# Two stages of a transformer kernel joined with the attentions that follow them, without a barrier between

## The chip, the cores and the metric

The kernel runs on 1 core of one Trainium2 chip. Its engines are TensorE (PE), VectorE (DVE), ScalarE (ACT), GpSimd (POOL) and SyncE (SP), which here issues every DMA. The time is that of the whole program on the device, in microseconds (us).

## What is computed

Two post-layernorm transformer layers on x of 8 x 512 x 128 (batch, positions, channels), 16 heads of 8 channels each. The reference, cut to what matters:

```
# layer 0: attention with relative positions
scores = einsum(Q, K) * scale + take(c2p, rel_pos) + swap(take(p2c, p2c_pos))
ctx = softmax(scores) @ V;  x = layernorm(x + ctx @ Wo.T + bo)
# layer 0: gated feed-forward over x and the x of one position earlier
x = layernorm(x + sigmoid(xr @ W_r) * (square(relu(xk @ W_k)) @ W_v))
# layer 1: attention with shifted sinusoids
scores = (QK' + u K' + rel_shift(Q r' + v r')) / sqrt(8)
x = layernorm(x + (softmax(scores) @ V) @ Wo + bo)
# layer 1: four hidden products with silu and gelu
x = layernorm(x + ffn(x))
```

## The kernel before

The program is five stages in a row, each a block of one instruction stream per engine: `opening_phase` (projections of layer 0), `attention_phase(0)`, `mixing_phase` (end of the first attention, feed-forward of layer 0, projections of layer 1; "dense part" in the change's name), `attention_phase(1)` and `dense_phase`. Between two stages stand `end_phase` and `start_phase`: all engines meet, SyncE clears every semaphore of the old stage (L89) and raises every one of the new stage by BASE (L81), and all engines meet again. In the program's order SyncE has 65, 48, 67 and 32 such clears at the four borders.

The opening stage goes over the 8 batches. PE projects a batch to queries, keys and values, ACT and DVE split the results into three bf16 parts, and SyncE writes them to DRAM: values (`write_values`, L169), stacks of the parts (`write_stack`, L174 and L177), offsets (L182), tables (L188). From the fourth batch on it also loads the stacks, tables and offsets of the first eight heads into `a_stks` and `a_tabs` (L193, L194, L232 to L235). Two buffers `o_part` hold the parts, so the next but one batch waits for a batch's writes (`stack_out`).

An attention goes over 128 heads (8 batches of 16), eight of them unrolled in a loop body. Per head and 128-row tile: PE makes scores in PSUM (L703, L705, in layer 0 also L709), DVE adds a band of position terms (L835) and takes the row maximum (L843), ACT exponentiates (L906), PE turns the tile (L724), ACT copies it (L913), PE weighs the values (L737). The band takes a way through DRAM that shifts each row. In layer 0: PE makes the key side (L744), DVE copies it (L853), SyncE writes it with one pitch (`shear_a`, L553) and reads it with another (L559), PE adds its turned form and the query side (`correction`, L751 and L752), ACT copies (L925), SyncE writes and reads again (`shear_b`, L565 and L571). In layer 1: PE makes the edges (L761), DVE copies them (L848), SyncE writes and reads (`shear_e`, L577 and L584). The band chain runs 5 to 7 heads ahead of the scores (`CORR_AHEAD`, `KEY_AHEAD`), the load of stacks 8 heads ahead. Before the first score, the chains of the first heads run alone.

The mixing stage is a pipeline of four batches: step i works on batches i+3, i+2, i+1 and i. Its last part (`tail`) rotates and splits the projections of batch i (L1380 to L1392 on DVE, L1237 and L1242 on ACT) and SyncE writes them: `write_stacks`, 15 DMAs a batch, for each of three groups of terms one for the keys (L1051) and four for query arrays (L1057), with rows of 512 bf16 elements. ACT's cast of the next but one batch waits until they have landed (`stack_written`).

What sets the order is the text of the program: each engine runs its stream in order, and SyncE has one queue. A DMA waits on that queue for the semaphore of its input, and everything behind it waits too.

## Time and profile before

| what | value |
|---|---|
| median of 3 runs (lowest, highest) | 2052.94 us (2052.21, 2053.58) |
| profiled execution, its time | 2053.05 us |
| its span, first to last instruction | 2051.2 us |
| PE, DVE, ACT busy | 84%, 71%, 72% of the span |
| DMA | 404.65 MB, 197 GB/s over the span |
| opening stage | 4.8 to 105 us, with the barrier behind it |
| first attention | 105 to 907 us |
| mixing stage | 907 to 1092 us |
| second attention | 1092 to 1704 us |
| dense stage | 1704 to 2051 us |

The spans of the stages are read from the first instruction behind each barrier. Busy time is summed over an engine's instructions; waits on semaphores, DMA issues and the clears and raises of semaphores are not in it, so a border between stages shows as time in which no engine is busy.

### The profile page before, as it was taken

To read this page: it belongs to the slowest core of one execution; us is meant where nothing else is said; L and a number is where in the kernel's file an instruction comes from. 1 tells how busy PE (TensorE), PEld (TensorE's weight loads), DVE (VectorE), ACT (ScalarE), POOL (GpSimd) and SP (SyncE) were. 2 spreads that over 40 slices of the span, in tenths; PEclk is the share of its full clock that TensorE was granted. 3 is DMA by queue.
4 is the path that set the end of the run, shared out by engine and by line. 5 is a ranking of instruction groups with operands and counts; after the bars stand their busy time and mean duration, and the time that the engine had idled before them with its cause. 6 is when DMAs were issued, how large, how long until landed. Compare 5 with 4: busy or idle time off the path is not lost. (4 is left out here: it accounts for less than half of the span.)

```text
span 2051.2 us, 44474 instructions
## 1 busy us (share of the span) xinstructions
PE 1728.5 (84%) x11694; PEld 1042.4 (51%) x11694; DVE 1454.1 (71%) x3499; ACT 1472.5 (72%) x2600; POOL 79.9 (4%) x102
## 2 busy tenths in 40 slices
PE   5269999999999999946743999999999995999998
PEld 2045555555555555524522555656565552454544
DVE  6358888888888888837973888988888873324322
ACT  4348888888888888836862999999999991223222
POOL 0000000000000000003510000000000000000000
PEclk8569999999999999977875999999999997999999
DMA  7678888888888888726996777777777744000100
GB/s 229 214 222 257 265 269 267 264 261 266 262 264 268 266 266 261 240 56 184 327 311 182 206 213 210 215 211 214 212 211 211 212 136 117 22 20 26 36 5 11
DMA packets 428234, 404.65 MB, mean 197 GB/s; under 512 B 38169, under 2 KB 348433, under 8 KB 428049
## 3 DMA queue, kind: packets, MB, share of 16 engines
q1 hardware_dynamic: 428177, 403.99, 65.6%
q8 instruction: 24, 0.39, 0.1%
...
HBM read 227.09 MB, written 176.29 MB: 197 GB/s over the span
## 5 line engine op out<-in xcount | busy, mean ns | idle before, releaser
L906 ACT ACTIVATE a_prob<-bank,a_negmax 128x512 f32<-128x512 f32 x1024 | 740.8, 723 | 47.3 <-DVE a_negmax L843 46.1
L843 DVE TENSOR_REDUCE a_negmax<-bank 128x1 f32<-128x512 f32 x1024 | 699.4, 683 | 0.3
L724 PE MATMUL bank<-a_ident,a_prob 128*128 128x128 f32 x4096 | 643.0, 280 | 56.2 <-ACT a_probt L913 48.3
L913 ACT COPY a_probt<-bank 128x512 f32<-128x512 f32 x1024 | 621.3, 607 | 90.4 <-PE bank L724 79.1
L724 PEld LDWEIGHTS bank<-a_ident,a_prob 128*128 128x128 f32 x4096 | 448.5, 141 | 171.7 <-issue 70.6
L835 DVE TENSOR_TENSOR bank<-bank,a_band 128x128 f32<-128x128 f32 (+3 forms) x1024 | 349.9, 342 | 69.6 <-PE bank L705 69.0
L703 PE MATMUL bank<-a_stks 74*128 74x192 bf16 (+7 forms) x1024 | 324.1, 317 | 10.4 <-ACT a_prob L906 10.1
L737 PE MATMUL bank<-a_probt,a_vs 128*32 128x512 f32 x2048 | 271.5, 604 | 14.9 <-ACT a_probt L913 14.9
L823 DVE COPY_PREDICATED bank<-a_mask,bank 128x128 f32<-128x128 uint32 (+1 forms) x512 | 139.6, 273 | 116.4 <-PE bank L709 114.0
L703 PEld LDWEIGHTS bank<-a_stks 74*128 74x128 bf16 (+1 forms) x1024 | 100.1, 98 | 235.3 <-ACT a_prob L906 200.4
L705 PE MATMUL bank<-a_stks 74*128 74x320 bf16 (+5 forms) x768 | 200.9, 262 | 0.0
L1676 DVE TENSOR_TENSOR d_drop<-bank,d_s 128x128 f32<-128x128 f32 x32 | 7.1, 284 | 170.4 <-PE bank L1599 170.4
L709 PE MATMUL bank<-a_stks 74*128 74x128 bf16 (+1 forms) x512 | 110.5, 216 | 10.9 <-DVE bank L823 2.6
L1578 PE MATMUL bank<-d_ha,d_h1T 128*128 128x512 f32 x256 | 112.3, 592 | 0.0
L751 PE MATMUL bank<-a_ident,a_sheared 128*128 128x128 f32 x512 | 106.4, 285 | 6.6 <-DMA a_sheared<-shear_a 5.1
L1578 PE MATMUL bank<-d_hb,d_h2T 128*128 128x512 f32 x256 | 111.2, 592 | 0.0
L925 ACT COPY a_corr<-bank 128x512 f32<-128x512 f32 x128 | 76.4, 597 | 42.9 <-PE bank L752 40.1
L848 DVE COPY a_corr<-bank 128x512 f32<-128x512 f32 x128 | 87.2, 681 | 16.7 <-PE bank L761 9.3
L752 PE MATMUL bank<-a_tabs,a_stks 65*128 65x128 bf16 x512 | 97.5, 225 | 0.0
L853 DVE COPY a_keyside<-bank 128x512 f32<-128x512 f32 x128 | 87.4, 683 | 13.3 <-PE bank L744 10.4
L761 PE MATMUL bank<-edges,a_stks 96*128 96x128 bf16 x512 | 51.0, 223 | 50.1 <-DMA a_ident<-in_ident 42.5
L1641 ACT ACTIVATE d_hb<-bank,d_fs 128x512 f32<-128x512 f32 x32 | 22.0, 687 | 90.6 <-PE bank L1578 90.6
...
## 6 DMA issues: line engine op xcount, KB each, us to landing
a_band<-shear_b SPq DMA_DIRECT2D x128, 512.0 KB, 5.0
shear_a<-a_keyside SPq DMA_DIRECT2D x128, 256.0 KB, 3.7
a_sheared<-shear_a SPq DMA_DIRECT2D x128, 256.0 KB, 3.7
shear_b<-a_corr SPq DMA_DIRECT2D x128, 256.0 KB, 2.8
shear_e<-a_corr SPq DMA_DIRECT2D x128, 256.0 KB, 2.2
a_band<-shear_e SPq DMA_DIRECT2D x128, 256.0 KB, 3.2
a_stks<-stack SPq DMA_DIRECT2D x256, 96.0 KB, 3.0
...
```

The costliest lines, as they stand in the source:

```text
L703: last = pe.matmul(score[:, 0:c], k[:, qlo, q], k[:, keys, 0:c], start=True, stop=True)
L705: last = pe.matmul(score[:, c:T], k[:, qhi, q], k[:, keys, c:T], start=True, stop=True)
L709: last = pe.matmul(other[:, 0:e - a], k[:, qhi, q], k[:, keys, a:e], start=True, stop=True)
L724: last = pe.transpose(turned_bank[k][:, n * 128:(n + 1) * 128], prob[h.slot % 2][:, n, k * 128:(k + 1) * 128], ident[:, :])
L737: pe.matmul(cbank[32 * j:32 * j + VW, :], vs[g][:, at:at + VW], probt[h.slot + j][:, k, :], start=(k == 0), stop=(k == NT - 1)).then_inc(p ...
L751: pe.matmul(corr_bank[:, q], sheared[h.slot % 4][:, q], ident[:, :], is_transpose=True, start=True, stop=False)
L823: v.copy_predicated(score[:, a:e], mask[:, 0:e - a], other[:, 0:e - a]).then_inc(fixed, 1)
L835: v.tensor_tensor(score[:, a:e], score[:, a:e], band[h.slot % bands][:, n, w:w + e - a], ALU.add).then_inc(added, 1)
L843: v.tensor_reduce(negmax[h.slot % 2][:, n:n + 1], score[:, :], AX.X, ALU.max, negate=True).then_inc(maxed, 1)
L906: nc.scalar.activation(prob[h.slot % 2][:, n, :], score[:, :], ACT.Exp, bias=negmax[h.slot % 2][:, n:n + 1]).then_inc(exped, 1)
L913: nc.scalar.copy(probt[h.slot][:, k, :], turned_bank[k][:, :]).then_inc(copied, 1)
L1578: last = pe.matmul(dst[:, :], w[:, k, 128 * m:128 * m + 128], src[:, k, :], start=(k == 0), stop=(k == KH - 1))
```

## The change

`opening_phase` and `mixing_phase` become `opening` and `mixing`, which no longer make a block of their own: each gives a program that is put into the same block as the attention behind it, engine by engine. The two `end_phase` and `start_phase` between them fall away; the semaphores of both are raised together ahead of the pair and cleared together behind it (SyncE then has 112 and 109 clears at the borders in front of the mixing and the dense stage). Buffers that only the stage ahead needs share memory (`arena`) with `prob` and `probt` of the attention.

The first heads' chains are written into the stage ahead. In the opening: stack and table loads from the fourth batch on, the products of key sides 0 to 3 after batches 5 and 6, their way through shear_a in batches 6 and 7, corrections after the last offset product. In mixing: stack loads of heads 0 to 7 behind batches 2 to 5 (two heads a batch), edges 0 and 1 in step 5 and 2 to 4 in step 6, all copied by ACT instead of DVE, and their writes and reads in steps 6 and 7. The stacks of the last mixing batch are written behind the first four heads of the second attention (`store_last`), and `settled` waits for all of the stage's writes after the fourth head.

Three more things: `stack1` has a row pitch of 5 x 512 + 32 elements and its query arrays are written as one row of 2049 elements instead of four of 512, 6 DMAs a batch for 15; the load of two rotated arrays is two pieces of 512 elements instead of one of 1024; and the second attention has 8 buffers each for edges and bands instead of 2 and 4.

The diff, cut to its core:

```diff
-ARRAYS = 5
+PITCH_S = 5 * T + 32
...
                     for b in range(B):
                         write_values(b)
+                        if b == 7:
+                            for j in (0, 1):
+                                att.shear_a_read(sp, j)
                         write_stack(b)
...
-                            if b > 3:
-                                first_head(2 * (b - 4))
-                                first_head(2 * (b - 4) + 1)
+                        if b > 2:
+                            for j in ((0, 1, 2), (3, 4), (5, 6), (), (7,))[b - 3]:
+                                att.head_load(sp, j)
+                        if b == 6:
+                            sp.wait_ge(filled, BASE + 16 * N_FILL)
+                            for j in (0, 1):
+                                att.shear_a_write(sp, j)
+                            att.offset_load(sp, 0)
+                        if b == 7:
+                            for j in (2, 3):
+                                att.shear_a_write(sp, j)
...
                     for b in range(B):
                         offset_product(b)
                         if b + 2 < B:
                             project(b + 2)
+                        if b == 5:
+                            pe.wait_ge(w_off_set, BASE + 2)
+                            for j in (0, 1):
+                                att.first_key(pe, j)
+                        if b == 6:
+                            for j in (2, 3):
+                                att.first_key(pe, j)
+                    pe.wait_ge(off_set, BASE + B)
+                    att.first_correction(pe, 0)
...
-            wide, bands = WIN if rel else REL, 4
+            wide, bands, corrs = (WIN, 4, 2) if rel else (REL, 8, 8)
...
+            def write_keys(sp, b):
+                sp.wait_ge(lo_set, BASE + 2 * b + 2)
+                for first_term, n, q in TERM_RUNS:
+                    sp.dma_start(stack[1][b, :, first_term:first_term + n, 0:T], part[b % 2][:, 0:n, KEYS:KEYS + T]).then_inc(stack_written[b % 2], 16)
+            def write_queries(sp, b, run):
+                sp.wait_ge(lo_set, BASE + 2 * b + 2)
+                first_term, n, q = TERM_RUNS[run]
+                same = bass.AP(part[b % 2][:, :, :].tensor, q * (WIDE + 2) + QV, [[3 * (WIDE + 2), C], [0, n], [1, 4 * T + 1]])
+                sp.dma_start(stack[1][b, :, first_term:first_term + n, T:5 * T + 1], same).then_inc(stack_written[b % 2], 16)
...
                         if tail is not None:
                             write_values(tail)
-                            write_stacks(tail)
+                        if tail == 6:
+                            for j in range(CORR_AHEAD - 1):
+                                att.edge_read(sp, j)
+                        if tail == 7:
+                            att.edge_read(sp, CORR_AHEAD - 1)
+                        if tail is not None and tail < B - 1:
+                            write_keys(sp, tail)
+                            for run in range(len(TERM_RUNS)):
+                                write_queries(sp, tail, run)
...
+                        if tail in (2, 3, 4, 5):
+                            att.head_load(sp, 2 * tail - 4)
+                            att.head_load(sp, 2 * tail - 3)
...
-            opening_phase(*kept)
-            end_phase()
-            attention_phase(0, kept)
-            end_phase()
-        mixing_phase()
+            start_phase()
+            with nc.Block() as block:
+                first.program(block)
+                att.program(block, first)
         end_phase()
...
+                mix.program(block)
+                att.program(block, mix)
```

Where the instructions stand now. SyncE's queue at the end of the opening stage and the start of the first attention, before (L182 offsets, L193 and L194 head loads, L89 the clears, L637 the mask, L553 and L559 write and read of shear_a):

```order
L182 DMA offsets<-o_off_part 4x16x1536
L193 DMA a_stks<-stack 48x2x512
L194 DMA a_stks<-stack 48x512
L193 DMA a_stks<-stack 48x2x512
L194 DMA a_stks<-stack 48x512
L182 DMA offsets<-o_off_part 4x16x1536
L89 ISA x65
L637 DMA a_mask<-in_mask 128x128
L553 DMA shear_a<-a_keyside 128x512 x2
L559 DMA a_sheared<-shear_a 128x512
L553 DMA shear_a<-a_keyside 128x512
```

After, from the last batch's values on (L599 and L600 are the head loads, L625 and L631 write and read of shear_a):

```order
L199 DMA values<-o_vt 128x4x144
L631 DMA a_sheared<-shear_a 128x512 x2
L204 DMA stack<-o_part 128x3072
L207 DMA stack<-o_part 128x1536
L207 DMA stack<-o_part 128x1024
L207 DMA stack<-o_part 128x512
L212 DMA offsets<-o_off_part 4x16x1536
L599 DMA a_stks<-stack 48x2x512
L600 DMA a_stks<-stack 48x512
L625 DMA shear_a<-a_keyside 128x512 x2
L631 DMA a_sheared<-shear_a 128x512 x2
L212 DMA offsets<-o_off_part 4x16x1536
```

The writes and reads of the first key sides stand between the last batch's own writes, no clear stands between them, and one head load is left there instead of four.

ACT in the mixing step of batch 6, before (L1258 rows of the last batch, L1237 and L1242 casts, L1210 a query copy):

```order
L1258 ACTIVATE m_x<-m_pre,m_shift,m_rstd 128x128 x4
L1237 CAST m_part<-m_full 128x1024
L1270 COPY m_xt<-bank 128x512
L1242 CAST m_part<-m_left 128x1538
L1210 ACTIVATE m_qv<-bank,m_uvs 128x512
```

and after (L722 are the copies of the first edges):

```order
L1367 ACTIVATE m_x<-arena,m_shift,m_rstd 128x128 x4
L722 COPY a_corr<-bank 128x512 x2
L1346 CAST m_part<-arena 128x1024
L1379 COPY arena<-bank 128x512
L722 COPY a_corr<-bank 128x512 x2
L1351 CAST m_part<-arena 128x1536
L722 COPY a_corr<-bank 128x512
L1319 ACTIVATE arena<-bank,m_uvs 128x512
```

Five copies of edges stand between the step's own instructions. SyncE's queue behind the last mixing step, before (L1051 and L1057 stacks of the three groups of terms, L532 to L535 the loads of head 0):

```order
L1051 DMA stack<-m_part 128x3x512
L1057 DMA stack<-m_part 128x3x512 x4
L1051 DMA stack<-m_part 128x2x512
L1057 DMA stack<-m_part 128x2x512 x4
L1051 DMA stack<-m_part 128x512
L1057 DMA stack<-m_part 128x512 x4
L89 ISA x67
L532 DMA a_stks<-stack 48x1536
L533 DMA a_stks<-stack 48x512
L534 DMA a_stks<-stack 48x512
L535 DMA a_stks<-stack 48x1024
```

and after, from the start of the attention's own part (L649 write of edges, L656 read of a band, L604 to L607 loads of a head, L1087 query rows of the last batch):

```order
L649 DMA shear_e<-a_corr 128x4x128
L604 DMA a_stks<-stack 48x1536
L605 DMA a_stks<-stack 48x512
L606 DMA a_stks<-stack 48x512
L607 DMA a_stks<-stack 48x2x512
L1087 DMA stack<-m_part 128x3x2049
L649 DMA shear_e<-a_corr 128x4x128
L656 DMA a_band<-shear_e 128x4x128
L604 DMA a_stks<-stack 48x1536
L605 DMA a_stks<-stack 48x512
L606 DMA a_stks<-stack 48x512
L607 DMA a_stks<-stack 48x2x512
```

The last batch's writes have moved behind the attention's own DMAs of its first heads, whose earlier loads stand several batches ahead.

## Rows read from the trace of the kernel before

**Rows 1.** Busy time by stretch: span, then engines, PE clock, DMA share, GB/s.

```profile
450.00:550.00 100.00, 93.34 (x740) 58.26 (x740) 85.54 (x220) 86.67 (x156) 0.00 (x0) 1.00 0.89 267
985.00:1000.00 15.00, 12.90 (x58) 9.17 (x58) 13.61 (x31) 11.94 (x22) 7.37 (x9) 0.77 1.00 334
1330.00:1430.00 100.00, 93.86 (x781) 59.92 (x780) 87.68 (x200) 98.13 (x185) 0.00 (x0) 1.00 0.73 212
1069.00:1083.00 14.00, 0.00 (x0) 0.00 (x0) 0.00 (x0) 0.00 (x0) 0.00 (x0) 0.50 1.00 342
85.00:88.00 3.00, 0.00 (x0) 0.00 (x0) 0.00 (x0) 0.00 (x0) 0.00 (x0) 0.50 1.05 387
```

**Rows 2.** Timeline, end of the opening: start us, us, engine, line, what [idle before].

```profile
82.11 0.68 DVE L372 TENSOR_TENSOR o_off_part<-o_off_left,o_off_part 64x512 bf16<-64x512 f32 x1 [0.68 <-ACT o_off_part L319]
83.87 0.43 SPq L169 DMA_DIRECT2D values<-o_vt  x1
...
92.56 0.54 SPq L182 DMA_DIRECT2D offsets<-o_off_part  x1
```

**Rows 3.** Timeline, start of the first attention.

```profile
105.51 0.58 PE L744 MATMUL bank<-a_stks,a_tabs 65*128 65x512 bf16 x1 [27.00 <-SPq L635]
108.27 1.73 SPq L553 DMA_DIRECT2D shear_a<-a_keyside  x2
110.34 0.32 SPq L559 DMA_DIRECT2D a_sheared<-shear_a  x1
...
117.32 0.44 SPq L553 DMA_DIRECT2D shear_a<-a_keyside  x1
121.22 0.32 SPq L559 DMA_DIRECT2D a_sheared<-shear_a  x1
...
125.65 0.45 PE L751 MATMUL bank<-a_ident,a_sheared 128*128 128x128 f32 x1 [2.90 <-DMA a_sheared<-shear_a]
126.95 0.37 PE L703 MATMUL bank<-a_stks 74*128 74x192 bf16 x1
129.56 0.69 ACT L906 ACTIVATE a_prob<-bank,a_negmax 128x512 f32<-128x512 f32 x1 [1.77 <-DVE a_negmax L843]
```

**Rows 4.** Marks of both barrier halves, L85 behind clears, L77 behind raises: times us.

```profile
L85 POOLq DRAIN  x4: 34/34/41, 97.6 to 1699.6; - x4
L85 SPq DRAIN  x4: 7/7/7, 101.6 to 1701.8; - x4
L77 POOLq DRAIN  x5: 34/34/41, 0.7 to 1702.0; - x5
L77 SPq DRAIN  x5: 7/7/7, 4.5 to 1704.1; - x5
```

**Rows 5.** Timeline of SP, ACT and DVE, end of the mixing stage.

```profile
1031.49 0.37 SPq L1051 DMA_DIRECT2D stack<-m_part  x1
...
1046.52 0.37 SPq L1051 DMA_DIRECT2D stack<-m_part  x1
...
1050.26 1.04 ACT L1237 CAST m_part<-m_full 128x1024 bf16<-128x1024 f32 x1 [0.83 <-DVE m_full L1381]
...
1060.15 1.47 ACT L1237 CAST m_part<-m_full 128x1538 bf16<-128x1538 f32 x1 [1.46 <-DMA stack<-m_part]
...
1065.49 2.90 DVE L1392 TENSOR_TENSOR m_part<-m_left,m_part 128x1538 bf16<-128x1538 f32 x2 [0.41 <-ACT m_part L1242]
...
1081.71 2.19 SPq L1057 DMA_DIRECT2D stack<-m_part  x4
```

**Rows 6.** Timeline of SP, PE and DVE, start of the second attention.

```profile
1092.38 0.35 SPq L532 DMA_DIRECT2D a_stks<-stack  x1
...
1100.53 0.61 PE L761 MATMUL bank<-edges,a_stks 96*128 96x128 bf16 x4 [42.49 <-DMA a_ident<-in_ident]
...
1112.68 0.49 DVE L835 TENSOR_TENSOR bank<-bank,a_band 128x128 f32<-128x128 f32 x2
```

**Rows 7.** The page's groups: ACT's copy of a correction in the first attention.

```profile
L925 ACT COPY a_corr<-bank 128x512 f32<-128x512 f32 x128 | 76.4, 597 | 42.9 <-PE bank L752 40.1
```

2312 lines of the change are left out of this document (1185 added, 1127 removed).

## The prediction

> **What bounds the kernel now.** I read the table by stretches first: how busy each engine is in one window of each stage [rows 1]. In the first attention (450 to 550 us) ACT and DVE are 87 and 86% busy, PE 93%; in the second (1330 to 1430 us) ACT is 98% busy. In the mixing stage (985 to 1000 us) DVE is busy 13.6 of 15 us and the DMA share is 1.00. So each stage is near a limit of its own and the change touches none of these loops' arithmetic. What is left is the seams, and there I read the timeline, at the two places where a stage ends and an attention starts.
>
> Seam one: the last engine work of the opening stage is a DVE instruction that ends at 82.8 us, SyncE's last DMA of that stage is issued at 92.6 [rows 2], and the attention's first product starts at 105.5, its first exponential at 129.6 [rows 3]. That is 46.8 us between the last engine work of one stage and the first exponential of the next. Seam two: DVE's last work of the mixing stage ends at 1068.4, SyncE still queues stack writes until 1083.9 [rows 5], the attention's first DMA is issued at 1092.4, its first product starts at 1100.5 and DVE adds the first band at 1112.7 [rows 6]. That is 44.3 us. Both together are 91 us, 4.4% of the run.
>
> **What the barriers cost, and what of that stays.** A barrier is three things here: waiting until the last DMA has landed, clearing every semaphore of the old stage, and raising every semaphore of the new one by BASE. The change keeps the number of semaphores nearly the same: SyncE's instructions show 65, 48, 67 and 32 clears before and 112 and 109 after. The clears are one instruction each and they are not hidden. From the queue's own marks [rows 4]: the first barrier's 65 clears run from 97.6 to 101.6 us, 4.0 us; the last one's 32 from 1699.6 to 1701.8, 2.2 us; so (4.0 - 2.2) / 33 = 0.055 us a clear. The first 65 raises run from 0.7 to 4.5 us, 3.8 us, the last 36 from 1702.0 to 1704.1, 2.1 us: 1.7 / 29 = 0.059 us a raise; I take 0.055 for both. This work does not vanish with the barrier, it moves:
> - ahead of the opening stage, 112 raises for 65: 47 x 0.055 = +2.6 us
> - after the first attention, 112 clears for 48: 64 x 0.055 = +3.5 us
> - ahead of mixing, 109 raises for 67: 42 x 0.055 = +2.3 us
> - after the second attention, 109 clears for 32: 77 x 0.055 = +4.2 us
>
> Together +12.6 us (9 to 15 at 0.04 to 0.065 us each), all on the path, since every engine waits at these barriers. The seams below are reckoned without them.
>
> **Seam one.** SyncE's queue is what is late here. In the last batch it issues values, four stacks, offsets, four head loads and offsets, 11 DMAs, from 83.9 us to 93.1 [rows 2], 0.84 us each. In the new order the same stretch up to the write of the fourth key side holds values, two reads of shear_a, four stacks, offsets, two head loads and two writes of shear_a: 12 DMAs, 10.1 us. Of the batches before it only batch 6 has another number of DMAs, two writes and three offset loads for four head loads, +0.8 us; batch 3 has six head loads in place of six offset loads. So values is issued at 84.7, the third key side is written at 93.1 and the fourth is out at 94.8. The engines' part is hidden under this queue: key products and DVE's key copies go where DVE waits for ACT and ACT for stack writes. The read of the third key side waits until its write has landed: 2.1 us from issue to issue in the trace (108.27 to 110.34 us) [rows 3], so about 95.2; two reads, an offset write and a write of shear_b, 0.3 to 0.5 us each as the issues of [rows 2, 3], put the fifth key side's write at 96.9. From there the old start-up chain is unchanged and I take it whole: write of that key side at 117.32, its read at 121.22, the fifth correction on PE at 125.65, the first score at 126.95, the first exponential at 129.56 [rows 3], 12.2 us. The first exponential comes at 109.1 instead of 129.6: -20.4 us. Bounds: if the whole start-up from the first write of shear_a (108.27 to 129.56, 21.3 us) ran only after the old queue's end at 93.1, it would come at 114.4: -15.2. If the read waits hid entirely, -25.
>
> **Seam two.** Nothing of the second attention waits for the seam any more: stacks of the first eight heads are loaded behind batches 2 to 5, their edge products and ACT's copies lie in batches 5 and 6, the last batch's stacks are written behind the first four heads. The score tiles of the first head can run as soon as PE has finished its projections; then DVE adds the first band right behind its last mixing instruction, ahead of which only the ACT additions push. Those are five copies of one bank, 0.597 us each by the same copy in the first attention [rows 7], 3.0 us, put into the step of batch 6. In that step ACT waited 0.83 us for DVE ahead of one cast and 1.46 us for stack<-m_part ahead of another [rows 5]. The first wait takes up 0.8 us of the copies; of the second I count half, since the writes that it waits for start as late as before. I take +1.5 us (0 to 3.0). Then the first band is added at 1068.4 + 1.5 = 1069.9 instead of 1112.7: -42.8 us. The activation table for the exponential is loaded while DVE finishes its last 2.9 us, as it now lies behind ACT's last cast. The last batch's 3.9 MB (15 DMAs of 128 rows and 512 elements each, 6 parts and 5 arrays) come on top of the attention's 212 GB/s at a DMA share of 0.73 [rows 1]; four heads at 4.5 us leave 18 us for 3.8 + 3.9 MB, which takes 22 us at 342 GB/s, the rate of pure stack writes [rows 1]. The 4 us fall into loads that are issued eight heads ahead and bands that are issued five ahead: cover of over 15 us, cost nothing.
>
> In the mixing steps themselves each of batches 2 to 5 gets eight head loads (0.67 MB). A step is 15.0 us long, from one batch's first stack write to the next (1031.5 to 1046.5) [rows 5]. Its DMA is 3.93 MB of stacks, 0.55 of values and rows, now 0.67 of heads: 5.15 MB. The trace bounds the rate: 342 GB/s where all rows are 1 KB, 387 GB/s in the opening's writes with rows of 1 to 6 KB [rows 1]. That is 15.1 or 13.3 us, and the new query rows are 4 KB. Batches 1 and 2, which also carry the next loads, need 5.64 and 6.08 MB: 16.5 and 17.8 us or 14.6 and 15.7. I take no cost, nearer to the fast rate; the other end is 79.6 us of DMA for five steps of 75, +5 us.
>
> A rule speaks against the new rows. The Trainium skill, page DMA: Bandwidth & Descriptors, section How a descriptor splits into AXI transactions, says that a row which does not start at a multiple of 256 bytes costs extra beats: a 576-byte one 25 in place of 18. The old pitch of 5120 bytes is such a multiple, the new one of 5184 is not. By that rule a 1 KB row would cost up to a quarter more, a 4 KB row about 6%: estimates from the page, of which no row of this trace shows anything; they would make the step 15.8 us of DMA and add some 3 us to the mixing stage.
>
> **Loops.** The bodies are the same instructions. With 9.25 ACT instructions a head the first runs 156 / 9.25 heads in 100 us, 5.93 us each, the second with 8.25 of them 4.46 [rows 1]. Eight buffers for edges and bands loosen waits of DVE and SyncE in the second attention, where ACT has 98% of the time: at most its idle 1.9 us in 100, over 580 us some 10, and I count none.
>
> **The sum**, against the profiled execution's 2053.05 us (span 2051.2; the median of the runs, 2052.94, is 0.1 lower): 2053.05 + 12.6 - 20.4 - 42.8 = 2002.4, taken as 2002.5 us, 2.5% faster. Extremes added: +9 - 25 - 44.3 = 1993 and +15 - 15.2 - 41.3 + 5 = 2016.5.
>
> **Rivals.**
> - Mixing gets bound by DMA. The share of 1.00 at 985 to 1000 us speaks for it, the 387 GB/s with long rows against. Price +5 us for the stage, and ACT's wait for stack writes grows by 1 to 3 us: 2008 to 2011.
> - Seam one only moves: SyncE's single queue holds the stage's own writes behind waits for landed key sides, and the start-up chain runs after it as before. For it: the queue has no gap in the last batches. Price: -15.2 for -20.4, 2008.
> - The second attention's loop gets a little faster, by ACT's idle time: 1992 to 1998. Against: no wait of ACT there is for a band.
> - Slower: the head loads of the second attention, now 1 KB pieces that start off the 256-byte grid and two pieces where one of 2 KB was, become so dear that DMA sets the loop. The loop uses 0.73 of DMA [rows 1], 3.25 us of a head's 4.45; the loads are 48 rows of 7 KB, 336 of the 945 KB that 212 GB/s move in a head's time, 1.2 us. To lose the 50.5 us gained, a head must take 0.4 us more, 4.85 us of DMA, so the loads would have to cost 2.8, 2.35 times as much. At three times as much the head takes 5.6 us: 2002.5 + 128 x 1.15 = 2150. The rule above gives a quarter more for them, 3.55 us a head, which changes nothing.
> - The change doesn't do what it says: the attention's first tiles wait after all until SyncE has written batch 6, because the bands' reads stand in that queue. They stand ahead of batch 6's stacks, so I give it little: at most 12 us of writes, 2014.
>
> **How the numbers follow.** Forecast 55%, with a range of its own of 1996 to 2009; mixing bound by DMA 17%; seam one only moved 11%; faster loop 8%; bands late 6%; slower 3%. Leaving out the slower case and the tails of the others, 1992 to 2015 holds 8 in 10. What a measurement here can tell from no change is about 0.2%, 4 us; all cases but the slower one lie more than 30 us below: faster 96%, within 0.2% 1%, slower 3%.
>
> **What would show it.** In the profile after: 112 and 109 clears, some 6 to 7 us each; the first exponential near 112 us of the new clock (109.1 + 2.6), the second attention's first band within 2 us of DVE's last mixing instruction, in place of 44.3; ACT's copies of a_corr in batch 6; stack writes with 4 KB rows during the first four heads of the second attention; mixing steps of 15 us; loops of 5.93 and 4.46 us a head as before. I am wrong if these loops change by over 1%, if the mixing steps are longer than 16 us, or if the exponentials of the second attention start later than 5 us after DVE's last mixing instruction.

## The result, and the profile after

The changed kernel takes 2017.95 us (median of 4 runs, 2013.47 to 2020.02) against 2053.01 before: a ratio of 0.9825, 95% interval 0.9811 to 0.9839. It is faster, as forecast, but by 35 us and not by 50.5. The 2002.5 us are missed by 15.5 us and the upper end of the range, 2015, by 3. The profiled execution took 2019.39 us with a span of 2017.6. Of all runs below one, the fourth of e2, took 2138.4 us at a granted TensorE clock of 0.78 instead of 0.95, and no median below has it.

A table by stretch says where. The marks are events that both traces have: the first DMA, the first exponential of the first attention, its last copy of outputs, the first DMA of the mixing stage, the first band added in the second attention, its last copy of outputs, the first DMA of the dense stage, the end; each mark is the start of its event. All are us.

| stretch | before | after | difference | forecast |
|---|---|---|---|---|
| raises ahead of the opening | 4.8 | 8.0 | +3.2 | +2.6 |
| opening to first exponential | 124.8 | 111.1 | -13.7 | -20.4 |
| rest of first attention | 767.1 | 765.7 | -1.4 | 0 |
| border to mixing | 10.6 | 16.9 | +6.3 | +5.8 |
| mixing to first band | 205.5 | 165.0 | -40.5 | -42.8 |
| rest of second attention | 583.9 | 591.2 | +7.3 | 0 |
| border to dense | 7.8 | 12.1 | +4.3 | +4.2 |
| dense | 346.9 | 347.7 | +0.8 | 0 |

The differences add to -33.6 us, which is that of the spans. (The forecast of -42.8 has 1.5 us of ScalarE's copies in it.) So 6.7 us are missing in the opening, of which the first attention returns 1.4, 7.3 in the first heads of the second attention, 2.3 in mixing, 1.2 in the semaphores, 0.8 in the dense stage: 16.9 us, what lies between 2019.39 and 2002.5. The dense stage spans 346.7 to 348.6 us in all the profiles below, so I read nothing into its 0.8.

The borders first, which answer to [rows 4]. Marks of both barrier halves of the changed kernel, L85 behind the clears, L77 behind the raises; first and last start:

```profile
L85 POOLq DRAIN  x2: 34/38/41, 887.9 to 1660.9; - x2
L85 SPq DRAIN  x2: 7/7/7, 894.5 to 1667.4; - x2
L77 POOLq DRAIN  x3: 34/34/41, 0.7 to 1667.6; - x3
L77 SPq DRAIN  x3: 7/7/7, 7.7 to 1669.7; - x3
```

112 clears run from 887.9 to 894.5 us, 109 from 1660.9 to 1667.4, and 112 raises from 0.7 to 7.7. That is 0.06 us each, 0.005 over what I took.

Seam one, answering to [rows 3]. Timeline of SyncE and ScalarE in the changed kernel; start, duration, what, and the idle time before it with what ended it:

```profile
97.60 0.83 SPq L625 DMA_DIRECT2D shear_a<-a_keyside  x2
101.97 0.95 SPq L631 DMA_DIRECT2D a_sheared<-shear_a  x2
...
103.63 0.39 SPq L637 DMA_DIRECT2D shear_b<-a_corr  x1
...
110.57 0.59 ACT L752 COPY a_corr<-bank 128x512 f32<-128x512 f32 x1 [11.98 <-DMA shear_b<-a_corr]
112.79 0.59 ACT L752 COPY a_corr<-bank 128x512 f32<-128x512 f32 x1 [1.64 <-PE bank L740]
116.76 0.59 ACT L752 COPY a_corr<-bank 128x512 f32<-128x512 f32 x1 [3.39 <-PE bank L740]
119.11 0.69 ACT L949 ACTIVATE arena<-bank,a_negmax 128x512 f32<-128x512 f32 x1 [1.76 <-DVE a_negmax L898]
```

A hop is one step of the chain through DRAM: the issue of a DMA, its landing, and the release of what waits for it. The fourth key side's write is out at 98.4 us, 98.0 by the forecast on this clock; the third's is issued at 97.60, where the forecast has 96.3. Then the read of the third waits until 101.97, 4.4 us after the write's issue, where I had 2.1. The first write of shear_b goes out at 103.63, and ScalarE, idle for 11.98 us in all, can copy the third correction only when it has landed, since there are two correction buffers: 6.9 us from issue to landing, 3.7 in the kernel before (116.84 to 120.5). The first exponential comes at 119.1, not 112.3.

Seam two, answering to [rows 5, 6]. ScalarE and VectorE at the end of mixing and the start of the second attention:

```profile
1048.97 1.50 ACT L1351 CAST m_part<-arena 128x1536 bf16<-128x1536 f32 x1
1052.41 0.59 ACT L722 COPY a_corr<-bank 128x512 f32<-128x512 f32 x1 [1.95 <-PE bank L713]
...
1064.82 1.28 ACT L949 ACT_TABLE_LOAD   x1
1067.81 2.28 ACT L949 ACTIVATE arena<-bank,a_negmax 128x512 f32<-128x512 f32 x3 [1.71 <-DVE a_negmax L898]
...
1055.71 1.23 DVE L1511 TENSOR_TENSOR m_part<-arena,m_part 128x1024 bf16<-128x1024 f32 x1 [3.46 <-ACT m_part L1351]
...
1063.88 2.89 DVE L1511 TENSOR_TENSOR m_part<-arena,m_part 128x1536 bf16<-128x1536 f32 x2 [0.40 <-ACT m_part L1351]
1066.69 0.49 DVE L890 TENSOR_TENSOR bank<-bank,a_band 128x128 f32<-128x128 f32 x2
```

The seam itself closed as forecast: VectorE adds the first band (L890) directly behind its last mixing instruction, and the exponential table is loaded meanwhile. In the step of batch 6, ScalarE waits 1.95 us for the product of the fifth edge tile ahead of its copy (L722), and VectorE 3.46 us for ScalarE. One earlier step is longer too. ScalarE and VectorE in the changed kernel, between the rotations of batches 3 and 4:

```profile
1011.21 1.47 ACT L1346 CAST m_part<-arena 128x1536 bf16<-128x1536 f32 x1 [1.85 <-DMA stack<-m_part]
...
1021.20 0.69 DVE L1480 TENSOR_TENSOR arena<-bank,arena 128x512 f32<-128x512 f32 x1 [3.95 <-PE bank L1246]
```

ScalarE waits 1.85 us until the stacks of batch 2 have landed, and VectorE, behind ScalarE and TensorE, 3.95 us. In the same step of the kernel before the waits are 0.23 and 1.67 us. The step lasts 17.8 us where it lasted 15.5; the other steps up to batch 5 last 14.9 to 16.4 us (15.0 to 16.3 before). It is 17.8 and 17.9 us in e1 and e7, and 18.7 in e10.

Then the first heads, by stretches of 20 us from the first band on, with the columns of [rows 1] (length of the stretch; busy us and instructions of PE, PEld, DVE, ACT and POOL, PEld being TensorE's weight loads; granted clock; DMA share; GB/s):

```profile
1066.00:1086.00 20.00, 16.06 (x91) 10.56 (x92) 17.99 (x42) 16.26 (x30) 0.00 (x0) 0.73 0.96 343
1086.00:1106.00 20.00, 16.31 (x130) 10.05 (x128) 12.46 (x29) 15.83 (x30) 0.00 (x0) 1.00 0.90 271
1106.00:1126.00 20.00, 17.34 (x131) 10.23 (x132) 16.50 (x38) 17.53 (x33) 0.00 (x0) 0.91 0.75 206
```

and the same from the kernel before:

```profile
1112.00:1132.00 20.00, 16.75 (x97) 10.45 (x95) 18.17 (x43) 16.64 (x30) 0.00 (x0) 0.76 0.68 177
1132.00:1152.00 20.00, 19.16 (x159) 12.19 (x158) 17.55 (x41) 19.73 (x38) 0.00 (x0) 1.00 0.68 197
1152.00:1172.00 20.00, 18.49 (x151) 11.60 (x149) 17.83 (x42) 19.64 (x38) 0.00 (x0) 1.00 0.76 217
```

ScalarE, which sets this loop, is busy 15.8 of 20 us in the second stretch where it was 19.7, and 17.5 in the third where it was 19.6: 6.0 us together. The DMA share is 0.96 and 0.90 in the first two stretches, against 0.68 and 0.68. VectorE's waits say for what:

```profile
1089.43 0.30 DVE L890 TENSOR_TENSOR bank<-bank,a_band 128x128 f32<-128x128 f32 x1 [2.67 <-DMA a_band<-shear_e]
...
1106.01 0.30 DVE L890 TENSOR_TENSOR bank<-bank,a_band 128x128 f32<-128x128 f32 x1 [2.96 <-DMA a_band<-shear_e]
...
1079.94 0.43 SPq L1087 DMA_DIRECT2D stack<-m_part  x1
...
1086.40 1.35 SPq L1087 DMA_DIRECT2D stack<-m_part  x1
...
1088.38 1.01 SPq L656 DMA_DIRECT2D a_band<-shear_e  x1
```

Two bands land late, at 1089 us among the writes of the last batch's stacks (L1087, the one at 1086.40 takes 1.35 us to issue), and at 1106 behind the last of them, issued at 1097.

### The profile page after: what moved, and what is told of

The parts are those of the page before. It is cut to its first block and busy times, and to the rows that moved or that the text cites. A ratio compares the mean times of both kernels' runs of the same rounds, so it can differ in the third digit from the quotient of the medians.

```text
span 2017.6 us, 44338 instructions
## 1 busy us (share of the span) xinstructions
PE 1726.7 (86%) x11694; PEld 1041.8 (52%) x11694; DVE 1447.8 (72%) x3492; ACT 1474.8 (73%) x2605; POOL 79.6 (4%) x102
## 5 line engine op out<-in xcount | busy, mean ns | idle before, releaser
L949 ACT ACTIVATE arena<-bank,a_negmax 128x512 f32<-128x512 f32 x1024 | 739.4, 722 | 34.6 <-DVE a_negmax L898 33.6
L813 PE MATMUL bank<-ident,arena 128*128 128x128 f32 x4096 | 644.3, 280 | 58.4 <-ACT arena L956 50.4
L956 ACT COPY arena<-bank 128x512 f32<-128x512 f32 x1024 | 620.1, 606 | 90.2 <-PE bank L813 77.8
L813 PEld LDWEIGHTS bank<-ident,arena 128*128 128x128 f32 x4096 | 449.7, 141 | 176.4 <-issue 71.4
L890 DVE TENSOR_TENSOR bank<-bank,a_band 128x128 f32<-128x128 f32 (+3 forms) x1024 | 350.0, 342 | 77.2 <-PE bank L794 69.5
L826 PE MATMUL bank<-arena,a_vs 128*32 128x512 f32 x2048 | 272.4, 606 | 14.9 <-ACT arena L956 14.9
L878 DVE COPY_PREDICATED bank<-a_mask,bank 128x128 f32<-128x128 uint32 (+1 forms) x512 | 139.5, 272 | 114.3 <-PE bank L798 112.3
L739 PE MATMUL bank<-ident,a_sheared 128*128 128x128 f32 x512 | 106.2, 285 | 20.4 <-DMA a_sheared<-shear_a 15.2
L1700 PE MATMUL bank<-d_ha,d_h1T 128*128 128x512 f32 x256 | 112.3, 592 | 0.0
L752 ACT COPY a_corr<-bank 128x512 f32<-128x512 f32 x128 | 76.4, 597 | 24.4 <-PE bank L740 12.3
L739 PEld LDWEIGHTS bank<-ident,a_sheared 128*128 128x128 f32 x512 | 74.1, 145 | 35.7 <-issue 23.2
L1768 ACT ACTIVATE d_hc<-bank,d_fs 128x512 f32<-128x512 f32 x32 | 22.0, 687 | 87.6 <-PE bank L1700 87.6
```

The costliest lines, as they stand in the source:

```text
L739: pe.matmul(corr_bank[:, q], sheared[h.slot % 4][:, q], ident[:, :], is_transpose=True, start=True, stop=False)
L813: last = pe.transpose(turned_bank[k][:, n * 128:(n + 1) * 128], prob[h.slot % 2][:, n, k * 128:(k + 1) * 128], ident[:, :])
L826: pe.matmul(cbank[32 * j:32 * j + VW, :], vs[g][:, at:at + VW], probt[h.slot + j][:, k, :], start=(k == 0), stop=(k == NT - 1)).then_inc(p ...
L878: v.copy_predicated(score[:, a:e], mask[:, 0:e - a], other[:, 0:e - a]).then_inc(fixed, 1)
L890: v.tensor_tensor(score[:, a:e], score[:, a:e], band[h.slot % bands][:, n, w:w + e - a], ALU.add).then_inc(added, 1)
L949: nc.scalar.activation(prob[h.slot % 2][:, n, :], score[:, :], ACT.Exp, bias=negmax[h.slot % 2][:, n:n + 1]).then_inc(exped, 1)
```

## The experiments

All are variants of the changed kernel, and e11 and e12 of e10. This is the table by stretch of all profiles (us; "start" is the first DMA; the middle columns are the stretches of the table above):

| | start | to first exp | attention 0 | border | to first band | attention 1 | border | dense | median |
|---|---|---|---|---|---|---|---|---|---|
| changed | 8.0 | 111.1 | 765.7 | 16.9 | 165.0 | 591.2 | 12.1 | 347.7 | 2018.0 |
| e1 | 8.0 | 110.1 | 765.4 | 17.0 | 163.7 | 584.5 | 12.2 | 346.7 | 2009.7 |
| e2 | 8.0 | 108.6 | 765.9 | 16.9 | 163.1 | 584.4 | 12.1 | 348.4 | 2009.3 |
| e3 | 8.0 | 111.8 | 764.9 | 16.9 | 164.5 | 590.6 | 12.1 | 347.8 | 2019.7 |
| e4 | 8.0 | 110.2 | 768.1 | 16.9 | 164.1 | 591.3 | 12.1 | 348.0 | 2016.4 |
| e5 | 8.0 | 100.5 | 768.6 | 16.9 | 164.8 | 590.0 | 12.1 | 348.6 | 2010.6 |
| e6 | 8.0 | 106.5 | 764.5 | 16.9 | 164.7 | 592.0 | 12.1 | 347.0 | 2012.1 |
| e7 | 4.5 | 108.9 | 766.2 | 10.1 | 162.4 | 590.1 | 7.5 | 347.7 | 2001.9 |
| e8 | 8.0 | 109.3 | 764.6 | 16.9 | 187.0 | 584.7 | 12.1 | 348.0 | 2032.3 |
| e9 | 8.0 | 111.4 | 766.8 | 16.9 | 171.5 | 595.2 | 12.1 | 347.3 | 2029.2 |
| e10 | 4.4 | 101.1 | 771.3 | 10.1 | 162.1 | 585.0 | 7.5 | 346.9 | 1987.9 |
| e11 | 4.4 | 100.9 | 772.6 | 10.1 | 161.4 | 586.0 | 7.5 | 348.5 | 1993.3 |
| e12 | 4.4 | 101.3 | 768.3 | 9.8 | 162.3 | 587.9 | 7.5 | 346.9 | 1989.2 |

Where a column's code is the same, its spread is what one profile can't tell apart: 108.6 to 111.4 us for the opening (changed, e1, e2, e4, e7, e8, e9), 163.1 to 165.0 for mixing (changed, e2, e3, e5, e6), 764.6 to 768.1 for the first attention (changed, e1, e2, e4, e7, e8, e9), 590.0 to 592.0 for the second (changed, e3, e5, e6, e7).

### The first heads of the second attention: e1, e2, e8

e1, the last batch's stacks left out (and zeros written there early in mixing):

```diff
-                        if not rel:
-                            before.store_last(sp, j)
```

> The changed kernel, with the stacks of the last mixing batch not written during the first four heads of the second attention; the rows of the last batch hold zeros instead, written by six DMAs early in the mixing stage (so the scores of the last 16 heads lack their data). Theory A (DMA backlog): the first heads of the second attention lose their time because the 3.9 MB of these stacks come on top of batch 6's 3.9 MB and of the attention's own 212 GB/s. Then the stretch from the first band (1066.7 us in the changed kernel) to the end of the attention (1660.9), 594.2 us there and 586.9 us before, shrinks by 5 to 7 us to 587 to 589, the waits of 2.67 and 2.96 us for a band at 1089 and 1106 us go, and the whole is 2011 to 2014 us where the changed kernel has 2018. Rival B (the slow first heads come from TensorE's lower clock and the order of the first tiles, not from DMA): the stretch stays at 593 to 595 us and the time at 2017 to 2019.

2009.7 us. The attention takes 584.5 us from the first band, 6.7 less than in the changed kernel and within 0.6 of the kernel before. e2 writes the same bytes, thinner:

```diff
-                    before.settled(sp)
-                    with sp.Fori(0, loops) as i:
+                    if not rel:
+                        for j in range(unroll):
+                            sync_step(sp, 0, FIRST + j, NHEAD)
+                            before.store_last(sp, FIRST + j)
+                    before.settled(sp)
+                    with sp.Fori(0 if rel else 1, loops) as i:
```

> The changed kernel, with the last mixing batch's stacks written in nine pieces over the first nine heads of the second attention instead of six over the first four (SyncE's first loop iteration written out). Theory A: the backlog spreads; at a DMA share of 0.73 the attention leaves some 92 GB/s of 342 free, 3.9 MB fit into 42 us, nine heads; the stretch from the first band to the attention's end falls from 594.2 us to 588 to 591, the time to 2012 to 2015 us. Rival B: no change, 2017 to 2019 us. If only batch 6's burst of 3.9 MB ahead of the first bands matters, this gains under 2 us while the variant without the last batch's stacks gains under 2 us as well.

584.4 us, 2009.3 us: as good as not writing them at all, and more than expected. Its first three stretches of 20 us:

```profile
1062.00:1082.00 20.00, 16.22 (x101) 10.41 (x102) 18.48 (x45) 17.47 (x31) 0.00 (x0) 0.79 0.96 329
1082.00:1102.00 20.00, 18.92 (x157) 11.88 (x154) 17.39 (x41) 19.73 (x38) 0.00 (x0) 1.00 0.96 298
1102.00:1122.00 20.00, 17.77 (x143) 11.04 (x144) 16.57 (x39) 18.48 (x35) 0.00 (x0) 1.00 0.95 270
```

The DMA share is 0.95 or 0.96 in all three, and ScalarE's second stretch is full again at 19.73. So it is not the bytes that cost 7 us but that they came faster than the loop's own use leaves room for. Theory A holds and B falls. Three more kernels below write these stacks the same way, and their second attention takes 585.0, 586.0 and 587.9 us: 0.5 to 4.0 us over the 583.9 of the kernel before, in four profiles. e8 goes the other way: the heads wait for all writes.

```diff
+                    if not rel:
+                        for j in range(FIRST):
+                            before.store_last(sp, j)
+                        before.settled(sp)
                     for j in range(FIRST):
                         sync_step(sp, 0, j, NHEAD, weighed=False)
-                        if not rel:
-                            before.store_last(sp, j)
...
+                    if not rel:
+                        before.settled(pe)
```

(and the same wait on VectorE and ScalarE)

> The changed kernel, with the waiting of the old barrier put back at seam two, without its clears and raises and with the first heads' chains still in the mixing stage: SyncE writes all stacks of the last batch first, and TensorE, VectorE, ScalarE and SyncE start the second attention when all of them have landed. The backlog is then gone when the heads start. Theory: the first band comes 3.9 + 3.9 MB behind, at 1083 to 1090 us instead of 1066.7, the attention then takes 587 to 588 us instead of 594.2, and the whole is 10 to 17 us slower than the changed kernel, 2028 to 2035 us: what is worth the most in seam two is that the first heads don't wait for the last writes. If the backlog is worth as much as the waiting, the time stays at 2018 to 2022.

2032.3 us. VectorE's first band:

```profile
1085.75 0.63 DVE L895 TENSOR_TENSOR bank<-bank,a_band 128x128 f32<-128x128 f32 x2 [23.65 <-PE bank L797]
```

The first band comes at 1085.8, 22.0 us later in the stretch, and the attention then takes 584.7 us, 6.5 less: 14.4 us of time. The overlap of the last writes is worth 22 us gross and 14 net as the change has it, and 23 with the writes thinned (2032.3 against 2009.3 us in e2).

### Seam one: e3, e5, e6

e3, SyncE doesn't hold its first shear_b writes behind the reads that wait for a landing:

```diff
+                    write_offsets(B - 1)
+                    att.shear_b_write(sp, 0)
+                    att.shear_b_write(sp, 1)
                     for j in (2, 3):
                         att.shear_a_read(sp, j)
-                    write_offsets(B - 1)
-                    att.shear_b_write(sp, 0)
                     att.shear_a_write(sp, 4)
-                    att.shear_b_write(sp, 1)
```

> The changed kernel, with SyncE's order at the end of the opening altered: the last offsets and the writes of the first two corrections to shear_b come before the reads of the third and fourth key side, which wait 3.5 us for a landing, instead of behind them. Theory C (seam one is late because SyncE's queue holds behind landings): the first shear_b write goes out at about 98.5 to 99.5 us instead of 103.6, and since it is what frees the two correction buffers, the first exponential of the first attention comes 3 to 5 us earlier than 119.1 us; time 2013 to 2015 us. Rival D (the chain is bound by DMA landings of 4 to 7 us however they are ordered): the first exponential at 118 to 120 us, time 2017 to 2019.

The first exponential comes at 119.79, time 2019.7: theory C, mine, fell, and rival D holds. The trace shows that the order did what it should, and nothing came of it:

```profile
98.13 1.46 SPq L637 DMA_DIRECT2D shear_b<-a_corr  x2
99.93 3.64 SPq L631 DMA_DIRECT2D a_sheared<-shear_a  x2
...
107.03 0.45 PE L739 MATMUL bank<-ident,a_sheared 128*128 128x128 f32 x1 [10.24 <-DMA a_sheared<-shear_a]
```

The shear_b writes are out at 98.1 to 99.6, some 5 us earlier, but the read of the third key side, issued at 99.93, now takes until 107.03 to reach the correction on TensorE (L739), 7.1 us; it was 101.97 to 104.72 in the changed kernel. What one hop gained, the next lost. The run has one thing besides: the last offsets, too, are now written ahead of the reads, and e6 will show that they matter. e5 takes the stage's own last writes out of the way:

```diff
                     att.shear_b_read(sp, 2)
+                    write_values(B - 1)
+                    write_stack(B - 1)
+                    write_offsets(B - 2)
+                    write_offsets(B - 1)
```

(and leaves them out where they stood)

> The changed kernel, with the opening stage's own last writes (values and stacks of the last batch, offsets of the last two) issued behind the chains of the first heads instead of among them. Theory G (each hop through DRAM in seam one takes 4 to 7 us instead of 2 to 4 because the stage's own writes are in the DMA engines): the hops become 2 to 4.5 us as in the kernel before, and the first exponential comes at 111 to 114 us instead of 116.6 to 119.8; some 1 to 3 us of it are given back in the first heads, where the 2.2 MB now fall: time 2012 to 2015 us. Rival H (hops are long for their own sake, in both kernels): the first exponential moves by under 2 us.

The first exponential at 108.52, more than forecast, and 2010.6 us:

```profile
90.56 0.83 SPq L630 DMA_DIRECT2D shear_a<-a_keyside  x2
93.55 0.94 SPq L636 DMA_DIRECT2D a_sheared<-shear_a  x2
94.60 0.37 SPq L642 DMA_DIRECT2D shear_b<-a_corr  x1
...
98.07 0.58 ACT L757 COPY a_corr<-bank 128x512 f32<-128x512 f32 x1 [2.44 <-DMA shear_b<-a_corr]
...
108.52 0.69 ACT L954 ACTIVATE arena<-bank,a_negmax 128x512 f32<-128x512 f32 x1 [1.76 <-DVE a_negmax L903]
```

Writes and reads of key sides are 3.0 us apart (90.56 to 93.55), ScalarE waits 2.44 us for shear_b, where it was 11.98. The first exponential is 8.0 to 10.8 us earlier than in the kernels with the changed opening (116.56 to 119.36). Of the 10.6 us to the changed kernel's profile 7.0 are SyncE's queue: the third key side is written at 90.56 instead of 97.60, since the values, stacks and offsets that SyncE issued from 89.3 to 95.4 us no longer stand ahead of it. From that write to the first exponential it takes 18.0 us instead of 21.5: 3.5 us are shorter landings and one write of offsets less on the way. In the kernel before, the same stretch takes 18.5 us (111.10 to 129.56). The first attention takes 768.6 us, 2.9 more than in the changed kernel but only 0.5 beyond the spread. e6 moves only the two writes of offsets, 384 of 2200 KB:

```diff
-                        if b > 0:
+                        if 0 < b < 7:
                             write_offsets(b - 1)
...
                     att.shear_b_read(sp, 2)
+                    write_offsets(B - 2)
+                    write_offsets(B - 1)
```

> The changed kernel, with only the writes of the last two batches' offsets (192 KB each) issued behind the first heads' chains. If a few engines of the 16 that carry these writes hold up what stands behind them, the shear_b write that takes 6.9 us to land in the changed kernel takes 3 to 4.5, and the first exponential comes 2 to 4 us earlier, 113 to 116 us. If the volume of all the stage's writes is the cause, under 1 us, 117 to 119.5.

114.45, 2.1 to 4.9 us earlier than with the changed opening, and 2012.1 us, as expected if these small writes hold up what is behind them out of proportion: their own issues are 1.5 us of it. The 1.8 MB of values and stacks are written as before, so volume isn't what costs most of it.

The traces hold one thing more, the single landing events of a DMA, of which what waits needs the last. In the changed kernel a write of 128 rows posts 16 of them, a write of offsets (64 rows of 3 KB) five: one 1.0 to 1.3 us after its issue, the other four 4.3 to 6.7 us after it. The first write to shear_b (us from its issue):

| | before | changed | e5 | e6 |
|---|---|---|---|---|
| eighth of 16 landing events | 3.0 | 2.7 | 3.0 | 3.0 |
| last | 3.7 | 6.9 | 3.4 | 3.6 |

In the seven profiles with the changed opening the eighth comes after 2.4 to 2.7 us and the last after 5.5 to 7.3. So half of a slow write lands as fast as ever and a few parts of it come late, while the last offsets, issued 0.65 us ahead of it in the changed kernel, are still landing (107.3 to 109.7 us; the write's last event is at 110.5). That these few parts share their DMA engines with the offsets fits both and isn't shown directly, as no record names the engine. Theory G holds in the main: the hops are long because of the stage's own writes, and of these it is the two small ones of offsets. From the third key side's write to the first exponential e6 takes 18.6 us, e5 18.0, the profiles of the changed opening 20.6 to 23.1.

### The semaphores and the copy order in mixing: e7

```diff
-                @block.sync
-                def _(sp):
-                    for handle in sems.values():
-                        sp.sem_clear(handle)
+                shares(block, lambda queue, handle: queue.sem_clear(handle))
...
-                        if tail == 6:
-                            att.first_edge_out(act, 4)
...
                             values_out(p)
+                            if tail == 6:
+                                att.first_edge_out(act, 4)
                             high(p, 0)
```

(`shares` gives every fifth semaphore to one of the five engines; the raises likewise)

> The changed kernel with two edits that lie in different places of the trace. One: the semaphores are cleared and raised by all five engines, a fifth each, instead of by SyncE alone. At 0.055 us each on SyncE, 112 take 6.2 us and 23 take 1.3: the two clearings shrink from 6.6 and 6.5 us to 1.5 to 2.5 and the raises from 7.0, some 6 and 2.1 to 2, 2 and 1 us, together 17 to 20 us less. If the semaphores are served one after the other whoever asks, nothing is gained. Two: ACT's copy of the fifth edge tile in the mixing step of batch 6 stands behind the step's own copies of queries and keys instead of ahead of them, where ACT waited 1.95 us for its product: the stretch from the end of the clearing to the first band, 170.4 to 172.2 us in five profiles, less its raises, shrinks by 1 to 2.5 us. Whole: 1998 to 2001 us.

2001.9 us. Start and borders fall by 3.5, 6.8 and 4.6, 14.9 us, less than the 17 to 20 expected, but more than the 13.8 that the change had added: the engines clear and raise at the same time. The second edit, in the step of batch 6:

```profile
1041.05 1.23 DVE L1513 TENSOR_TENSOR m_part<-arena,m_part 128x1024 bf16<-128x1024 f32 x1 [1.39 <-ACT m_part L1353]
```

VectorE waits 1.39 us where it waited 3.46, 2.07 us less (and the same 1.39 or 1.40 in e10 and e12, which have this edit). The kernel before had this step 2.1 us shorter than the changed one (12.04 us between the rotations of batches 5 and 6, 14.14 after), and e7 has 12.06 again. So ScalarE's 3.0 us of copies cost nothing; where one of them stood did, as it put two of TensorE's own products (L1252, L1254) ahead of what ScalarE waited for.

### Layout of stack1: e4, e9

```diff
-PITCH_S = 5 * T + 32
+PITCH_S = 5 * T + 128
```

> The changed kernel, with a pitch of stack1's rows of 5 x 512 + 128 elements, 5376 bytes, a multiple of 256, instead of 5184, which is none. Theory E (rows that start off the 256-byte grid cost more, as the Trainium skill has it, page DMA: Bandwidth & Descriptors, section How a descriptor splits into AXI transactions): the mixing stage, 165.1 us from its start to the first band in the changed kernel, gets 1 to 3 us shorter, and the DMA share of the second attention's loop falls from 0.73 by 0.02 or more. Rival F (the grid costs nothing here): 164.5 to 165.5 us and 0.73, time 2017 to 2019 us.

164.1 us to the first band, inside the spread, and a DMA share of 0.75 in the loop where it was 0.73: rival F. A pitch off the 256-byte grid costs nothing here that a run can tell, with query rows of 4 KB; query rows of 1 KB at both pitches were not compared.

e9 undoes the long rows:

```diff
-                same = bass.AP(..., q * (WIDE + 2) + QV, [[3 * (WIDE + 2), C], [0, n], [1, 4 * T + 1]])
-                sp.dma_start(stack[1][b, :, first_term:first_term + n, T:5 * T + 1], same)...
+                for at in range(0, 4 * T, T):
+                    wide = T + (at == 3 * T)
+                    same = bass.AP(..., q * (WIDE + 2) + QV + at, [[3 * (WIDE + 2), C], [0, n], [1, wide]])
+                    sp.dma_start(stack[1][b, :, first_term:first_term + n, T + at:T + at + wide], same)...
```

> The changed kernel, with the query arrays of stack1 written in four pieces of 512, 512, 512 and 513 elements each, 15 DMAs a batch as before, instead of one row of 2049. Pitch and contents are the changed kernel's. If long rows keep the mixing steps, which now carry the head loads too, from being bound by DMA (1 KB rows moved 342 GB/s, rows of 1 to 6 KB 387 in the kernel before), the stretch from the mixing stage's first DMA to the first band, 163.1 to 165.0 us in the profiles so far, grows by 3 to 8 us, and the backlog behind it costs the first heads 1 to 2 us more: 2022 to 2028 us. If the long rows do nothing, 163 to 165.5 us and 2016 to 2020.

2029.2 us, 11 more and 1 beyond what I expected: 6.5 in mixing and 4.0 in the second attention. Both kernels in mixing, the changed one first:

```profile
1006.00:1021.00 15.00, 9.59 (x50) 7.31 (x48) 11.18 (x22) 10.23 (x18) 8.54 (x8) 0.77 1.06 363
1021.00:1036.00 15.00, 10.74 (x51) 7.02 (x50) 11.92 (x20) 12.84 (x22) 4.85 (x4) 0.89 0.94 334
```

```profile
1006.00:1021.00 15.00, 7.62 (x37) 5.12 (x36) 12.11 (x27) 8.83 (x16) 8.54 (x8) 0.77 1.03 307
1021.00:1036.00 15.00, 9.04 (x41) 5.62 (x40) 12.01 (x20) 12.21 (x21) 4.99 (x4) 0.80 0.94 301
```

In these stretches the DMA moves 301 and 307 GB/s with rows of 512 elements and 334 and 363 with rows of 2049; in the other full stretches of e9 it moves 319 to 332 (981 to 996 us, 323; 997 to 1012, 332; 1016 to 1031, 319; 1033 to 1048, 329). ScalarE then waits for the stacks' landing step by step:

```profile
1014.13 1.47 ACT L1348 CAST m_part<-arena 128x1536 bf16<-128x1536 f32 x1 [3.82 <-DMA stack<-m_part]
...
1047.68 1.47 ACT L1348 CAST m_part<-arena 128x1536 bf16<-128x1536 f32 x1 [1.54 <-DMA stack<-m_part]
...
1065.07 2.42 ACT L1348 CAST m_part<-arena 128x1536 bf16<-128x1536 f32 x2 [3.42 <-DMA stack<-m_part]
```

e9's short rows start off the 256-byte grid, unlike those of the kernel before. How much of the 11 us is the rows' length and how much their start isn't separated: that takes e9 at the pitch of e4, which wasn't run.

### Together: e10, e11, e12

e10 is e2, e5 and both edits of e7 in one kernel.

> Four edits of the runs so far together: the opening's own last writes behind the first heads' chains, the mixing stage's last stacks over nine heads, all five engines clearing and raising semaphores, the fifth edge copy later. They lie in different stretches, so the table by stretch should add: 4.5 to the first DMA, 100.5 to the first exponential, 768.6, a border of 10.1, 162.4 to 164, 584.4, a border of 7.5, 347.5, in all 1985.5 to 1987 us of span, 1987 to 1990 us of time. If one edit's gain was only moved behind (the backlog of one stretch met in the next), more than 1992.

1987.9 us, a ratio of 0.968 to the kernel before (0.9664 to 0.9697) and 30 us under the changed one. The stretches add up, but for the first attention: 771.3 us, 5.6 more than in the changed kernel and 2.6 more than in e5, which writes the same there. In e11 the opening's last writes go out in pieces behind each of the first four heads.

```diff
                         sync_step(sp, 0, j, NHEAD, weighed=False)
-                        if not rel:
-                            before.store_last(sp, j)
+                        before.store_last(sp, j)
...
+                    def store_last(sp, j):
+                        if j == 0:
+                            write_values(B - 1)
+                            write_offsets(B - 2)
...
```

> As the joined kernel, with the opening's own last writes in pieces behind each of the first four heads of the first attention instead of all at once ahead of them. In the variant with these writes in one piece the first attention took 768.6 us from its first exponential where five profiles of the changed opening show 764.9 to 768.1. If the burst of 2.2 MB costs the first heads 1 to 3 us, pieces bring 766 to 767 and the whole is 1 to 2 us below the joined kernel; if not, the same within 1 us.

1993.3: worse, 5.4 us above e10, against the forecast. The first attention takes 772.6 us, 1.3 more than in e10; the rest of the 5.4 isn't explained. The stall only moved (second and fourth stretch of 10 us, from the first exponential on; e10 first, e11 second):

```profile
115.50:125.50 10.00, 6.57 (x56) 4.92 (x53) 7.39 (x20) 7.62 (x15) 0.00 (x0) 0.98 0.76 239
135.50:145.50 10.00, 9.31 (x74) 5.44 (x73) 8.34 (x22) 8.57 (x16) 0.00 (x0) 1.00 0.94 286
```

```profile
115.40:125.40 10.00, 8.87 (x72) 6.48 (x71) 9.91 (x26) 9.69 (x19) 0.00 (x0) 1.00 0.92 299
135.40:145.40 10.00, 6.33 (x49) 3.85 (x47) 5.88 (x16) 6.16 (x11) 0.00 (x0) 0.92 0.66 208
```

VectorE, 9.7 of 10 us busy there in the changed kernel's second stretch, is 7.4 in e10, and 5.9 in e11's fourth. e12 has pieces of 128 to 288 KB over eleven heads.

```diff
+                    bounds = {3: (0, 2), 4: (2, 3), 5: (3, 5), 6: (5, 6), 7: (6, 8), 8: (8, 9), 9: (9, 11), 10: (11, 12)}
...
+                            for a, at, src in terms[slice(*bounds[j])]:
+                                sp.dma_start(stack[0][B - 1, a, :, at, :], part[(B - 1) % 2][:, src, :])...
```

> The joined kernel, with the opening's own last writes cut into pieces of 128 to 288 KB over the first eleven heads of the first attention (SyncE's first loop iteration written out there too). In the joined kernel this attention takes 771.3 us from its first exponential, 5.6 us more than in the changed kernel (765.7), and its second stretch of 10 us has DVE busy for 7.4 us where it is 9.7 in the changed kernel. The loop's DMA share is 0.87, so it leaves some 45 GB/s: 2.2 MB want 49 us, eight heads. If a burst beyond what the loop leaves is what costs the 5.6 us, the attention now takes 765 to 768 us and the whole is 1982 to 1986 us against 1987.9. If it is TensorE's clock, which starts its rise from the same low level with less work ahead of the first head, it stays at 770 to 773 us and the time at 1987 to 1990.

The first attention takes 768.3 us, 3.0 less and 0.3 above the forecast, but the second, whose code is e10's, 587.9, 2.9 more, and the time, 1989.2, is e10's and misses the 1982 to 1986. VectorE waits for bands in its first heads, 2.52 us at the longest. Why these fell worse than in e10, with the same writes behind the same heads, stays open; so does whether the last 2.6 us of the first attention are burst or TensorE's clock, whose granted mean is 0.50 in the first ten microseconds of the attention in both and 0.55 in the changed kernel.

## Why the prediction was wrong, point by point

**Semaphores, right.** +12.6 forecast, 13.8 measured, by the price of 0.06 us.

**Seam one, the mis-sized term.** -20.4 forecast, -15.1 measured (-13.7 and the -1.4 behind it). On the new clock the first exponential was due at 112.3 us and came at 119.1. Of these 6.8 us 1.3 are the third key side's write, issued that much later than I had it (the fourth was right to 0.4). The step that failed is the two prices behind it. "2.1 us from issue to issue" measured 4.4, and "from there the old start-up chain is unchanged and I take it whole, 12.2 us" measured 15.0 (104.13 to 119.11); 0.5 more went into the four DMAs between them. The 2.1 us are the kernel's very first hop, at a DMA share of 0.10 or less from 98 to 109 us; the third key side's own hop took 3.1 us in the kernel before (111.10 to 114.16) and takes 3.0 in e5, so 0.9 of the 2.3 was there to be read. The rest of it, and the chain's 2.8, come with the stage's own last writes: without them e5's chain takes 12.3 us (96.26 to 108.52), and of the 3.5 us by which the whole stretch from the third key side's write gets shorter in e5, moving the two small writes of offsets alone gives 2.9 (e6). A full DMA is not the cause: the 12.2 us had a mean DMA share of 1.00 (117 to 129.5 us of the kernel before), the 15.0 one of 0.81 (104 to 119). My rival, "seam one only moves", had the size (-15.2) but by the queue's order, and e3, which changes the order within the chain, gained nothing.

**Seam two, right.** The first band follows VectorE's last mixing instruction at once; e8 shows what the wait would have cost.

**ScalarE's copies, right size by luck.** +1.5 forecast (0 to 3), 2.1 measured. It was not the copies' time but the wait for the fifth product, which I hadn't in the sum (e7).

**The last batch's writes, wrong.** The second step that failed: "cost nothing" was 7.3 us. I had the numbers: 7.7 MB in 18 us is 4 us more than fit at 342 GB/s, and the 3.9 MB of batch 6, issued at 1063 to 1067 us, were missing from that sum. I then set the excess against loads issued eight heads ahead. But a head's edges are written and its band read only four to five heads ahead, through the same engines as the stacks, and behind them in one queue: two bands came late. e1 and e2 show it from two sides.

**Mixing isn't DMA-bound, right but for one step.** The forecast's sign of being wrong, a mixing step over 16 us, came: one takes 17.8 us for 15.5, as ScalarE waits 1.85 us for the landing of batch 2's stacks, within the 1 to 3 us of my rival. That step is 2.3 us, the fifth product 2.1, and the other steps give 0.5 back, in all 3.9 where I had 1.5. With rows of 1 KB two steps take 18.9 and 16.9 us and the rival's case comes true whole, 6.5 us more where I had given it 5 (e9, by their length or their start off the grid). The rule of the Trainium skill (DMA: Bandwidth & Descriptors, How a descriptor splits into AXI transactions) on rows off the grid, by which I had some 3 us, doesn't show in any run here (e4).

**Loops, right.** 5.93 and 4.46 us a head as before; a faster second attention didn't come.

**The range.** Each bound was taken around one term, and no rival said that at both seams the old stage's last writes are in the way of what the new stage waits for, though [rows 1] showed shares of 1.00 and 1.05 right ahead of them. That moved two terms the same way: most of the 5.3 us at seam one and the 7.3 at seam two, of 17 us.

## What to carry to other kernels

Where two stages are joined, the price of a round trip through DRAM at the seam must be read beside the writes that will be there, and a chain of such trips multiplies the difference. Writes that nobody needs soon belong behind those that someone waits for, even small ones, and in pieces that fit into what the loop leaves. For the second attention, 3.9 MB over four heads cost 7 us, over nine heads 0.5 to 4. When work is put into another engine's idle time, look at what it waits for itself, not only at how long it takes.

## What the runs showed that I hadn't expected

- A 256 KB DMA can take 7 us to land while the engines are far from full on average. Between 94 and 108 us of the changed kernel the writes to shear_b took up to 7.2 us, at a mean DMA share between 0.27 and 0.86 in stretches of 2 us from 98 to 110. The Trainium skill (DMA: Bandwidth & Descriptors, Anatomy of one DMA) gives 2.0 us plus the bytes at 436 GB/s for DMAs that GpSimd issues, an estimate of 2.6 us for this size. Here SyncE issues them; the 2.1 us at the idle start of the attention before are near that, the 4.4 and 6.9 us at the seam are not.
- Two writes of 192 KB of offsets cost 2.1 to 4.9 us of the chain (e6), while volume alone, at 342 GB/s, would be 1.1. Behind them a write's eighth landing event is on time and its last 2 to 4 us late.
- Engines can clear and raise semaphores side by side: 112 took 6.6 us on one engine, and the whole border from the last output copy to the next DMA went from 16.9 to 10.1 us with five (e7).
- 1 KB rows moved 301 to 332 GB/s in the full stretches of mixing (e9) and 4 KB rows up to 363 (changed kernel); on the 256-byte grid 1 KB rows moved 334 and 342 in the kernel before [rows 1].
